# Turning the second gate's weighted ranks on VectorE instead of TensorE

## The reference, cut to what matters

```
logits = x @ W_router.T                  # 8 experts
w      = softmax over the top 2 logits, 0 for the other six
mid    = einsum(x, lora_A)               # 8 experts x rank 16 = 128 "ranks" per token
mid    = mid * w[..., None]
out    = base(x) + einsum(mid, lora_B)   # 128 ranks -> 1024 columns
```

## Time and profile before

| | |
|---|---|
| median of 3 runs | 889.35 us (888.65 to 889.44) |
| the profiled execution | 889.4 us, its span 887.2 us |
| TensorE busy | 882.7 us (99%) |
| VectorE busy | 714.5 us (81%) |
| ScalarE busy | 324.3 us (37%) |
| GpSimd busy | 156.5 us (18%) |
| DMA | 191.93 MB, mean 216 GB/s |
| granted TensorE clock | 1.0 of full speed throughout |

### The profile page before, as it was taken

One profiled execution on the slowest core, in us unless ns is written; L12 is line 12 of the kernel. 1 busy time (PEld: TensorE's weight loads), 2 busy tenths in 40 slices (PEclk: granted clock), 3 DMA queues, 4 the chain that ended last, 5 costly groups with the idle time before them and its releaser, 6 DMA issues.

```text
span 887.2 us, 13623 instructions
## 1 busy us (share of the span) xinstructions
PE 882.7 (99%) x4566; PEld 773.3 (87%) x4566; DVE 714.5 (81%) x1587; ACT 324.3 (37%) x525; POOL 156.5 (18%) x310
## 2 busy tenths in 40 slices
PE   9999999999999999999999999999999999999998
PEld 8999998888998888888888888888888888888787
DVE  6999999786787968989787877877877877877875
ACT  6688878421424434232322222222222222222221
POOL 0210120111011002313202302302302312312300
PEclk9999999999999999999999999999999999999999
DMA  9533340785312042575786887887887987987976
GB/s 349 213 98 114 125 137 25 245 258 174 120 49 95 3 141 76 173 285 209 237 295 252 297 287 259 298 299 245 302 294 248 304 278 261 305 287 252 304 230 233
DMA packets 62609, 191.93 MB, mean 216 GB/s; under 512 B 8256, under 2 KB 12742, under 8 KB 60620
## 3 DMA queue, kind: packets, MB, share of 16 engines
q1 hardware_dynamic: 50282, 158.92, 50.6%
q0 software_dynamic: 11968, 31.88, 12.9%
q10 hardware_dynamic: 290, 0.26, 0.1%
HBM read 158.80 MB, written 32.76 MB: 216 GB/s over the span
## 4 chain that ended last, share of the span: by engine, by line
PE 97%; DMA 2%; SPq 0%; DVE 0%; ACT 0%; issue 0%; DVEq 0%
PE bank L941 16%; PE bank L593 15%; PE bank L594 15%; PE bank L595 15%; PE bank L965 8%; PE bank L923 7%; PE bank L909 5%; PE bank L969 4%; PE bank L1064 2%; PE bank L749 2%; PE bank L918 2%; DMA t_lo<-t_scratch 1%; PE bank L637 1%; PE bank L858 1%; PE bank L644 1%; DMA m_raw<-m1t 1%
## 5 line engine op out<-in xcount | busy, mean ns | idle before, releaser
L941 PE MATMUL bank<-g_hi,xs 128*128 128x512 f32 x440 | 146.9, 395 | 0.0
L556 POOL DMA_DIRECT2D p1sel<-p_scratch x128 | 65.6, 512 | 289.6 <-issue 289.6
L941 PEld LDWEIGHTS bank<-g_hi,xs 128*128 128x128 f32 x440 | 81.7, 188 | 15.7
L965 PE MATMUL bank<-t_hi,xs 128*128 128x512 f32 x336 | 90.9, 392 | 0.0
L941 PE MATMUL bank<-g_lo,xs 128*128 128x512 f32 x220 | 86.7, 394 | 0.0
L1141 ACT ACTIVATE xs<-x_raw 128x1024 fp32r<-128x1024 f32 x60 | 61.8, 1054 | 51.8 <-PE bank L969 50.2
L1514 DVE TENSOR_TENSOR xs<-x_raw,xs 128x1024 fp32r<-128x1024 f32 x60 | 73.2, 1242 | 7.4 <-ACT xs L1141 7.0
L593 PE MATMUL bank<-gx,xs 128*128 128x304 f32 x256 | 78.5, 307 | 0.0
L595 PE MATMUL bank<-gx,xs 128*128 128x304 f32 x256 | 77.4, 302 | 0.0
L594 PE MATMUL bank<-gx,xs 128*128 128x304 f32 x256 | 77.2, 301 | 0.0
L965 PEld LDWEIGHTS bank<-t_hi,xs 128*128 128x128 f32 x336 | 63.0, 188 | 14.3 <-DMA t_hi<-t_scratch 0.3
(11 more groups left out here) (395 smaller groups left out, 2124.3 us busy)
## 6 DMA issues: line engine op xcount, KB each, us to landing
t_hi<-t_scratch SPq DMA_DIRECT2D x82, 512.0 KB, 5.6
t_lo<-t_scratch SPq DMA_DIRECT2D x82, 512.0 KB, 6.5
x_raw<-xq SPq DMA_DIRECT2D x16, 1024.0 KB, 8.6
out<-ost SPq DMA_DIRECT2D x63, 256.0 KB, 8.3
p1sel<-p_scratch POOLq DMA_DIRECT2D x64, 192.0 KB, 6.0
w_raw<-wall SPq DMA_DIRECT2D x15, 512.0 KB, 4.6
w<-e_scratch SPq DMA_DIRECT2D x6, 1024.0 KB, 5.1
ea<-e_scratch POOLq DMA_DIRECT2D x8, 644.0 KB, 5.3
```

What stands on the lines that cost most here:

```text
L556: pool.dma_start(f(p1sel[b][64 * s:64 * s + STK, cs]), p1_dram[bass.ds(i * STK, STK), cs]).then_inc(sems[b], 16)
L941: mm = nc.tensor.matmul(bk[j][:], l[:, c, :], m[:, c, :], start=first and c + k == 0, stop=c + k == KH + 1, skip_group_check=True)
L965: nc.tensor.matmul(bk[j][:], x[u][:, c, :], t_hi[:, c, :], start=first and c + u == 0, stop=False, skip_group_check=True)
```

## The change

In tiles 2 to 14, TensorE makes no `mid_turn` and waits only for `mid_s`, since the token product behind it overwrites what the second gate reads. VectorE gets 16 transposes behind `back`: for each 32 tokens g and each 32 ranks k one instruction on both halves b (32 partitions x 2 x 32 values), which reads `midv` in SBUF and writes TR in PSUM. Ahead of them it waits for `mid_s` and, from tile 2 on, for ScalarE's copy out of TR (`m0r_s`). The last raises `t2_mm`. Tiles 0, 1 and 15 turn on TensorE as before.

```
@@ winograd_products (TensorE)
                 product(60, 1, quarter(1, 0, 1), g_quarter(1, 1), True)
 
-                mid_turn(tau)
+                pe.wait_ge(mid_s, tau + 1)
                 x_product(tau + 1, (0,))
@@ VectorE
+            def mid_turn(tau):
+                v.wait_ge(mid_s, tau + 1)
+                if tau >= REG:
+                    v.wait_ge(m0r_s, tau - REG + 1)
+                turned = TR[:, 0:T2].rearrange("p (b t) -> p b t", b=2)
+                for g in range(P // SX):
+                    ts = slice(SX * g, SX * g + SX)
+                    for k in range(P // SX):
+                        ks = slice(SX * k, SX * k + SX)
+                        ins = nc.vector.transpose(turned[ks, :, ts], midv[ts, :, ks])
+                ins.then_inc(t2_mm, 1)
@@ VectorE, the loop over the Winograd tiles
                 back(tau)
+                if tau + 1 < NT2:
+                    mid_turn(tau)
```

## The result

The changed kernel takes 891.9 us (median, 891.61 to 892.25) against 889.17 us for the kernel before, measured beside it: a ratio of 1.003 with a 95% interval of 1.0021 to 1.004. It is slower by 2.7 us, inside the range that was given and on the slower side of the 0.2% line, where the likeliest forecast, 890.0 us, was not. The profiled execution took 891.68 us, with a span of 889.5 us.

A forecast was written before the change was run, and what follows sets the result against it. TensorE, busy 99% of the span, was taken to bound the kernel. A 1.4 us gain in common tiles and 2.0 us loss in the first gave +0.6 on 889.4, so 890.0 us; range 887.7 to 894.0.

The forecast's parts named there:

- TensorE's saving: Tiles 2 to 14: two transposes fewer on TensorE save 0.21 us a tile, 2.7 us at most over 13 tiles.
- The place of the cost: VectorE's longer chain behind line 2020 makes m0 late for TensorE's turn; gate 0.29 us late in the common tile shown.
- The pace of the transposes: VectorE's 16 transposes into PSUM start 0.248 us apart, with no PSUM surcharge, 3.98 us of VectorE per tile.
- B: Rival: slower PSUM writes or later m0 lengthen VectorE's chain; 894.3 us at 0.270 us a transpose; chance 0.30.
- The slack at the turn: Before TensorE's turn of m0: m0 could come 0.26 us later at no cost, 0.20 and 0.32 as ends.
- A: Main forecast: the 16 VectorE transposes run one after another at about 0.248 us; 890.0 us, 888.6 to 891.2; chance 0.50.
- The first tile: First Winograd tile: VectorE has least waiting to absorb the transposes, so m0 is late and 2.0 us are lost.
- The common tiles: The 12 later Winograd tiles: TensorE's 12 x 0.21 us less 1.1 us of waits for m0, a 1.4 us gain.
- The sum: Whole kernel: -1.4 + 2.0 = +0.6 us against the profiled 889.4 us, so 890.0 us.
- C: Rival: the 16 VectorE transposes overlap like small products, 0.135 us apart; 887.0 us; chance 0.12.
- D: Rival: TensorE has more slack at the late gate, so only the first Winograd tile pays; 888.7 us; chance 0.08.
- Other engines: ScalarE's later high parts arrive in time for VectorE; x loads 0.3 us late, 2.2 in the first tile, still in time.

## Why the prediction was right and where it was not

**TensorE's saving, 0.21 us a tile.** Right: 32.93 against 33.14 us in every tile of the run with one transpose.

**The place of the cost.** Right. The wait sits at the turn of m0, in the common tiles it averages 0.18 us, about as large as the saving, and the first tile has too little cover. The waits before the sum and the gate are gone, as forecast. The chain from line 2020 to the gate was computed as 13.59 us; with transposes into SBUF it is 13.60.

**The pace of the transposes.** This is the step that failed. I took 0.248 us, with no surcharge for PSUM, from the sums of the earlier trace rows (290 ns into PSUM, 292 into SBUF). The transposes start 0.270 us apart, and the run into SBUF puts the difference on the destination. 15 x 0.022 = 0.33 us a tile, which is just 13.92 - 13.59. The prediction had named another duration into PSUM as a sign that it would be wrong, and a common tile over 33.2 us as the sign of B; five of the twelve were. So it was the mechanism of rival B, at the very pace to which I had set its end, 0.270, and B was given 0.30. A sum is a poor stand-in for a transpose: what a destination costs one operation says little of another.

**The slack at the turn.** Mis-sized the other way. I counted 0.26 us from m0's readiness, 0.32 at most. The rows after show that m0 may be ready 0.06 us ahead of its turn (0.05 to the load, 0.01 from load to turn), where it was 0.50 us before (0.27 to the load in the earlier trace rows, 0.23 from the load to the turn): 0.44 us. I had charged most of the usual 0.23 us between load and matmul as necessary. It is not. In the running stream the load starts together with the matmul ahead of it and its own matmul 0.23 us later; the load may start later than that at no cost. The run into SBUF shows it: m0 is ready at 696.07 + 0.42 = 696.49, 0.19 us ahead of its turn, the load comes 0.13 us ahead, and the turn still stands 0.23 us behind the matmul at 696.45:

```profile
696.07 0.42 DVE L1984 TENSOR_TENSOR ranks_raw<-bank,rt 128x256 f32<-128x256 f32 x1
```
```profile
696.55 0.28 PEld L859 LDWEIGHTS bank<-pk,ranks_raw 128*128 128x128 f32 x2
```
```profile
696.45 0.39 PE L942 MATMUL bank<-g_lo,xs 128*128 128x512 f32 x1
696.68 0.38 PE L859 MATMUL bank<-pk,ranks_raw 128*128 128x128 f32 x2
```

This is why B came out at 891.9 us and not at its 894.3: some 0.18 us less in each of 13 tiles is 2.3 us.

**Range and luck.** The measured time lies in the stated range, but outside A's own (888.6 to 891.2), and the answer that it held likeliest, no change, did not come. The two errors work against each other; had only the pace been off, the sum would have gone to B's 894.3, out of the range. That it stayed inside owes something to luck.

**The first tile.** Forecast 2.0 us of loss. With the measured pace and slack it would be 1.97 + 0.33 - 0.18 = 2.12 us; the profile has 2.26. The other 0.14 us is no cost of the change: the second gate, ahead of the first vector transpose, ended that much later in this execution. Line 2020 starts 442.85 - 429.45 = 13.40 us behind the turn of m0, against 442.55 - 429.29 = 13.26 before:

```profile
442.85 0.42 DVE L2020 TENSOR_TENSOR ranks_raw<-bank,rt 128x256 f32<-128x256 f32 x1
```

The other runs bear this out. With the loops nested the other way it starts 13.27 us behind, and the tile takes 35.28 us, 2.14 lost. Into SBUF it starts 13.65 us behind: 2.12 - 0.33 + 0.39 = 2.18 us, and the 35.34 us measured are 2.20 lost. So the faster transposes helped there too, and a late second gate hid it. On the way TensorE waited for line 2229's sum and for line 2132's (now 2243 and 2144), as written; they were stages of the one delay:

```profile
456.44 0.50 PE L1064 MATMUL bank<-p1sel,lowt 114*128 114x512 f32 x1 [0.83 <-DVE p_sum L2243]
...
460.55 0.50 PE L923 MATMUL bank<-k_hi,srk_hi 128*128 128x512 f32 x1 [0.77 <-DVE p_sum L2144]
```

**The common tiles.** Forecast a gain of 1.4 us, measured 0.16. The slower pace alone would have made them cost 2.5 us or so (12 x 0.33 less the 1.4); the larger slack gave most of it back.

**The sum.** +0.6 us was forecast and +2.7 measured: 1.2 us from the common tiles and 0.3 from the first. Another 0.16 us had passed before the first turn of m0 (429.45 against 429.29), which makes the 2.3 us of the profiled pair; the medians differ by 0.4 more, which no profile explains.

**Rivals C and D** fell: the transposes don't overlap (4.30 us for 16), and all tiles but one paid, not the first alone. D's premise, that TensorE has more slack than I read, was true, but the slower pace used it up.

**Other engines.** ScalarE's later high part of the ranks and the later load of x cost nothing that shows; between 400 and 870 us TensorE waited for a transfer once, for 0.3 us.

## What to carry to other kernels

When work is moved off a busy engine to one with idle time, add up the chain on the receiving engine from the moved work to the next thing that the busy engine takes from it, and set that against the waits along this chain; the idle share says nothing (VectorE was at 89% in tiles with no gap on TensorE, and at the same load in tiles with one). Look at the first pass of a loop by itself, since one-time work there may have eaten the cover, and leave it as it was if so. And when a producer is put later to shorten such a chain, look at what stands behind its store in the DMA queue: here that took back most of the gain (1.1 us of 3.75 were left) until it was moved too.

## What the hardware showed that was not expected

A 32x64 float32 transpose on VectorE takes 256 ns into PSUM and 236 ns into SBUF, 0.270 and 0.250 us from start to start ((4.30 - 0.256) / 15 and (3.98 - 0.236) / 15), while 128x128 sums took 290 and 292 ns. A TensorE weight load that waits for its data can be followed by its matmul within 0.01 us of its start, though the two are 0.23 us apart in the running stream behind a 512-column matmul.
